# The last two batches' pages computed behind quad 34, sums in the order of completion, and four gathers a quad

## What is computed

```python
x = x + xattn(layernorm(x), ctx)
h = layernorm(x)                                  # 4096 tokens x 128
shared = silu(h @ sg_w.T) * (h @ su_w.T) @ sd_w.T
scores = sigmoid(h @ gate_w.T) + gate_bias        # 64 experts in 8 groups
# the 4 best groups, in them the 6 best experts, weights scaled to sum 1 -> comb
a = silu(einsum('th,eih->eti', h, eg_w)) * einsum('th,eih->eti', h, eu_w)
routed = einsum('eti,ehi,te->th', a, ed_w, comb)
out = x + shared + routed
```

## Time and profile before

| | us |
|---|---|
| median of the runs (592.63 to 596.7) | 593.04 |
| span of the profiled execution, first to last instruction | 792.4 |
| POOL busy in it | 389.3 |
| PE busy | 503.3 |
| DVE busy | 456.1 |
| ACT busy | 352.3 |

### The profile page before, as it was taken

One profiled execution on the slowest core, in us unless ns is written; L12 is line 12 of the kernel. 1 busy time (PEld: TensorE's weight loads), 2 busy tenths in 40 slices (PEclk: granted clock), 3 DMA queues, 4 the chain that ended last, 5 costly groups with the idle time before them and its releaser, 6 DMA issues.

```text
span 792.4 us, 12061 instructions
## 1 busy us (share of the span) xinstructions
PE 503.3 (64%) x3204; PEld 420.8 (53%) x3204; DVE 456.1 (58%) x2264; ACT 352.3 (44%) x962; POOL 389.3 (49%) x425
## 2 busy tenths in 40 slices
PE   3767555766555574632359956788688889777700
PEld 2445334444334343311359856778688789777700
DVE  6587556667555576656233624576776756346532
ACT  3564433344443343322215934466666766246400
POOL 2006445654455655556650055454554545555574
PEclk9885555555555555555568976899988876897555
DMA  7532123322123332223425533455455555654421
GB/s 195 194 113 94 62 100 107 104 100 98 47 80 107 107 100 98 95 78 129 124 81 134 148 94 95 106 138 151 126 145 137 151 137 146 160 153 107 113 70 47
DMA packets 98708, 90.60 MB, mean 114 GB/s; under 512 B 10576, under 2 KB 85456, under 8 KB 98640
## 3 DMA queue, kind: packets, MB, share of 16 engines
q1 hardware_dynamic: 85232, 64.26, 27.5%
q0 software_dynamic: 12288, 25.29, 11.3%
q10 hardware_dynamic: 1120, 0.28, 0.2%
HBM read 41.32 MB, written 48.46 MB: 113 GB/s over the span
## 4 chain that ended last, share of the span: by engine, by line
PE 30%; another core or an unknown queue 17%; issue 16%; ACT 14%; POOL 11%; DVE 9%; ACTq 2%; DMA 0%; POOLq 0%; DVEq 0%
PE bank_s L1155 14%; POOL pages L447 6%; PE bank_o L1155 4%; PE bank_q L1155 3%; PE bank_s L1151 2%; ACT d_now L511 2%; ACT p_t L533 2%; ACT pxt L511 2%; POOL empty L492 2%; ACT gu_now L511 2%; ACT k_exp L521 1%; ACT s_act L672 1%; POOL p_t L492 1%; PE bank_o L1151 1%
## 5 line engine op out<-in xcount | busy, mean ns | idle before, releaser
L1155 PE MATMUL bank_s<-pxt,gu_now 128*128 128x64 f32 x768 | 116.5, 316 | 51.6 <-ACT pxt L511 31.3
L492 POOL DMA_INDIRECT p_t<-results,place_i x96 | 91.1, 949 | 110.6 <-ACT s_act L672 72.8
L1155 PEld LDWEIGHTS bank_s<-pxt,gu_now 128*128 128x128 f32 x768 | 111.4, 231 | 58.1 <-ACT pxt L511 36.4
L492 POOL DMA_INDIRECT empty<-results,place_i x96 | 91.1, 949 | 77.2 <-issue 35.1
L1111 DVE TENSOR_TENSOR h_t<-bank_s,s_act 64x256 f32<-64x256 f32 x128 | 54.7, 427 | 113.9 <-ACT s_act L672 95.4
L447 POOL DMA_INDIRECT pages<-payload,place_i x96 | 93.0, 968 | 37.9 <-issue 27.0
L447 POOL DMA_INDIRECT pages<-payload_b,place_i x96 | 92.8, 967 | 35.8 <-issue 26.7
L437 POOL TENSOR_TENSOR rstd<-ve,minus_half 128x4 f32<-128x4 f32 (+1 forms) x21 | 18.6, 885 | 132.6 <-DVE ve L927 130.0
L672 ACT ACTIVATE s_act<-bank_s 64x512 f32<-64x512 f32 x64 | 37.8, 590 | 79.5 <-remote 36.0
L533 ACT ACTIVATE p_t<-bank_s 128x512 f32<-128x512 f32 x64 | 36.2, 598 | 67.9 <-issue 27.9
L1255 PE MATMUL bank_o<-bias_h,row_h 96*128 96x256 bf16 x16 | 6.1, 381 | 72.2 <-ACT o_t L511 70.3
(11 more groups left out here) (169 smaller groups left out, 1164.1 us busy)
## 6 DMA issues: line engine op xcount, KB each, us to landing
pg<-pages SPq DMA_DIRECT2D x64, 258.0 KB
results<-y_s SPq DMA_DIRECT2D x64, 256.0 KB
pages<-empty SPq DMA_DIRECT2D x21, 774.0 KB
w_gu<-in_expert_gu SPq DMA_DIRECT2D x16, 256.0 KB
w_d<-in_expert_d SPq DMA_DIRECT2D x31, 128.0 KB
out_x<-xb SPq DMA_DIRECT2D x16, 128.0 KB
xb<-in_x SPq DMA_DIRECT2D x3, 512.0 KB, 8.0
pages<-payload,place_i POOLq DMA_INDIRECT x96
```

What stands on the lines that cost most here:

```text
L492: pool.indirect_dma_start(out=ys[n % YS_SLOTS][:, k, :], out_offset=None, in_=results[0:landed * QUAD * P, :], in_offset=bass.IndirectOffs ...
L1155: return pe.matmul(dst, w, v, start=True, stop=True)
```

## The change

- Quads are now computed in another order. `quad_at(p)` gives the quad that stands at position p of the loop: positions 0 to 34 are quads 0 to 34, positions 35 to 48 are the fresh quads 50 to 63, and positions 49 to 63 are quads 35 to 49. Below, a *position* counts in the new order; in the kernel before, position and quad are the same.
- `landed_before(b)` says how many positions must be stored for batch b: 11 + 3b for batches 0 to 8 (11 to 35), 46 for batch 14, 49 for batch 15, and 52, 55, 58, 61, 64 for batches 9 to 13. `turn_of` sorts the batches by it: 0 to 8, 14, 15, 9 to 13. Gathers, sums, the shared expert and the stores of the output go in this order.
- Four gathers are tied to each quad in place of three, and a batch starts with the quad behind its last one: `gathers_from` is 12, 15, 18, ... 36 for batches 0 to 8, then 47, 50, 53, 56, 59, 62, 65. The sums of its two tiles stand behind the products at `gathers_from` + 3 and + 4.
- `pages` and `results` are two tables each, an old and a new one. The tables are filled with zeros in 22 DMAs as before, of other sizes (the old table's first has 8 pages, the new one's 8).

```diff
-FIRST_BEAT = FIRST_SUM - 6
-GATHERS_A_QUAD = TOPK // 2
+GATHERS_A_QUAD = 4
+FRESH_AT = 35
+FRESH_QUADS = NQ - SPLIT_QUAD
...
+        def quad_at(p):
+            if p < FRESH_AT:
+                return p
+            return p - FRESH_AT + SPLIT_QUAD if p < FRESH_AT + FRESH_QUADS else p - FRESH_QUADS
+
+        def landed_before(b):
+            n = quads_before(b)
+            if b >= SPLIT:
+                return n - SPLIT_QUAD + FRESH_AT
+            return n if n <= FRESH_AT else n + FRESH_QUADS
+
+        turn_of = sorted(range(B), key=landed_before)
+        gathers_from = []
+        for b in turn_of:
+            gathers_from.append(max(landed_before(b) + 1, gathers_from[-1] + TPB * TOPK // GATHERS_A_QUAD if gathers_from else 0))
+
+        def summed_at(p):
+            return [TPB * i + t for i in range(B) for t in range(TPB) if gathers_from[i] + 3 + t == p]
...
-                if q == SPLIT_QUAD:
+                if q == FRESH_AT:
                     pages_complete(B)
...
-                if q == FIRST_STORE + 2 * TPB * stored:
+                if q == gathers_from[stored] + 4 + STORE_BEHIND + 2:
                     store(stored)
...
-            def beat(step):
+            def beat(i, step):
                 q, part = divmod(step, GATHERS_A_QUAD)
+                q += gathers_from[i]
+                if q >= NQ:
+                    return
                 if part == 0:
                     pool.wait_ge(act_ready, q + 1)
                 elif part == 1:
+                    pool.wait_ge(pxt_ready, min(q + 2, NQ))
+                elif part == 2:
                     pool.wait_ge(h_ready, HALVES * (q + 1))
                 else:
                     pool.wait_ge(y_ready, q)
...
                 for k in range(TOPK):
-                    if GATHERS_A_QUAD * FIRST_BEAT + TOPK * n + k < GATHERS_A_QUAD * NQ:
-                        beat(GATHERS_A_QUAD * FIRST_BEAT + TOPK * n + k)
-                    pool.indirect_dma_start(out=ys[n % YS_SLOTS][:, k, :], out_offset=None, in_=results[0:landed * QUAD * P, :],
-                                            in_offset=bass.IndirectOffsetOnAxis(ap=place_i[:, n, k:k + 1], axis=0)
+                    beat(i, t * TOPK + k)
+                    pool.indirect_dma_start(out=ys[n % YS_SLOTS][:, k, :], out_offset=None, in_=done,
+                                            in_offset=bass.IndirectOffsetOnAxis(ap=place_i[:, tile, k:k + 1], axis=0)
...
             def combine_next(q):
-                n, odd = divmod(q - FIRST_SUM, 2)
-                if n >= 0 and not odd:
+                for n in summed_at(q):
                     combine(n)
...
-            for n in range((NQ - FIRST_SUM + 1) // 2, TPB * B):
-                combine(n)
+            for n in range(TPB * B):
+                if gathers_from[n // TPB] + 3 + n % TPB >= NQ:
+                    combine(n)
```

More of the change, by code:

```diff
@@ L81, with build @@
 POWER_AFTER = {}
-def build(nc, x, ctx_cols, wq, bq, wk, bk, wv, bv, wo, bo, gate_cols, gate_bias, expert_gu, expert_d, shared_gu, shared_d, out, pages, results):
+def build(nc, x, ctx_cols, wq, bq, wk, bk, wv, bv, wo, bo, gate_cols, gate_bias, expert_gu, expert_d, shared_gu, shared_d, out, old_pages, new_pages, old_results, new_results):
     with ExitStack() as ctx:
@@ L272, in quads_before, with quad_in, held @@
             return pages_before(b) // QUAD
-        def fills_before(b):
-            return 1 + (pages_before(b) - FIRST_FILL + FILL - 1) // FILL
-        def held(q):
+        def quad_at(p):
[13 more added lines that the diff above has]
+            return [TPB * i + t for i in range(B) for t in range(TPB) if gathers_from[i] + 3 + t == p]
+        def fills_before(b):
+            if b < SPLIT:
+                return 1 + (pages_before(b) - OLD_PAGES % FILL + FILL - 1) // FILL
+            return OLD_FILLS + 1 + (pages_before(b) - OLD_PAGES - NEW_PAGES % FILL + FILL - 1) // FILL
+        def quad_in(both, p):
+            q = quad_at(p)
+            new = q >= SPLIT_QUAD
+            at = q - SPLIT_QUAD if new else q
+            return both[new][at:at + 1, :, :, :]
+        def held(p):
+            q = quad_at(p)
             for start in (0, SPLIT_QUAD):
@@ L332, in prefill @@
             def prefill(k):
-                sp.wait_ge(prefilled, 16 * (k + 1))
-                sp.dma_start(fill_v[bass.ds(k, 1), :, :].rearrange("k p c -> (k p) c"),
-                             empty[:, :, :].rearrange("p r c -> p (r c)")).then_inc(prefilled, 16)
+                new = k >= OLD_FILLS
+                pages, i = (new_pages, k - OLD_FILLS) if new else (old_pages, k)
+                first = (NEW_PAGES if new else OLD_PAGES) % FILL
+                start = 0 if i == 0 else (first + (i - 1) * FILL) * P
+                rows = first if i == 0 else FILL
+                if k > 0:
+                    sp.wait_ge(prefilled, 16 * k)
+                sp.dma_start(pages[start:start + rows * P, :].rearrange("(p r) c -> p (r c)", p=P),
+                             empty[:, 0:rows, :].rearrange("p r c -> p (r c)")).then_inc(prefilled, 16)
             load_x(0)
@@ L446, in scatter @@
                 for k in range(first, after):
-                    pool.indirect_dma_start(out=pages[:, :], out_offset=bass.IndirectOffsetOnAxis(
+                    pool.indirect_dma_start(out=(new_pages if n >= SPLIT else old_pages)[:, :], out_offset=bass.IndirectOffsetOnAxis(
                         ap=place_i[:, TPB * n + t, k:k + 1], axis=0), in_=payload[n % 2][:, t, k, :],
@@ L481, in gather @@
             def gather(n):
-                landed = quads_before(n // TPB)
-                if n % TPB == 0:
+                i, t = divmod(n, TPB)
+                b = turn_of[i]
+                tile = TPB * b + t
+                done = (new_results[0:(quads_before(b) - SPLIT_QUAD) * QUAD * P, :] if b >= SPLIT
+                        else old_results[0:quads_before(b) * QUAD * P, :])
+                landed = landed_before(turn_of[i])
+                if t == 0:
                     for j in range(SLOTS):
@@ L1094, in combine @@
                         dve.wait_ge(added, (TOPK - 1) * n + k)
-                    part = dve.scalar_tensor_tensor(out=xt, in0=ys[n % YS_SLOTS][:, k, :], scalar=weight[:, n, k:k + 1], in1=xt,
+                    part = dve.scalar_tensor_tensor(out=xt, in0=ys[n % YS_SLOTS][:, k, :], scalar=weight[:, tile, k:k + 1], in1=xt,
                                                     op0=ALU.mult, op1=ALU.add)
```

45 lines of the change are left out of this document (23 added, 22 removed).

## The result

The change makes the kernel slower: 623.85 us (median of 4 runs, 621.08 to 626.69) against 593.56 us (4 runs, 592.63 to 596.7), a ratio of 1.0503 with a 95% interval of 1.045 to 1.0555, or +30.3 us. The profiled execution of the changed kernel took 625.98 us, with a span of 624.1.

A forecast was written before the change was run, and what follows sets the result against it. The prediction took POOL's indirect DMAs as the bound. Its second stage went from 249.5 to 276.7 us, +27 us; it took +20, between +27 and +12, so 593 + 20 = 613 us, range 583 to 622, likeliest case 602 to 620.

The forecast's parts named there:

- The bound: Whole kernel: POOL's indirect DMAs bind it, 192 scatters at 1.27 us and 192 gathers at 1.25 us.
- Balanced: Second stage of the kernel before: DVE and POOL both come to 250 us, the loop to 203 us.
- The gap: Between batches 8 and 14: POOL stands still from 136.3 to 163.5 us after the first gather, 27 us.
- the two upper ones: Second stage, two estimates of the loss: +27 us at the trace's spacing, +12 us at 1.15 us.
- an upper value: Second stage: the +27 us sum, called upper since the spacing without the profiler may be shorter.
- item 1 of the parts: End of the kernel: 16 gathers follow the last quad instead of 27; a time bound by POOL gains nothing.
- item 4: Behind the pause: 84 gathers, 105 us, to 276.7 us; other bound, 17 positions at 5.0 us, called lower.
- Item 5: Order, two tables, fills and two more waits in a group: taken as 0, between -2 and +2 us.
- The profiled span: Changed kernel's profile: the span may shrink by up to 16 us, even opposite to the median.
- Faster: Rival, loop and end: quads have slack, the gap costs nothing, only the end counts; 582 us, chance 0.23.
- Same: Rival, gap and end: spacing near 1.0 us, some DVE slack, the two cancel; 588 to 598 us, chance 0.2.
- Much slower: Rival, loop: POOL stalls reach DVE at once through the sums and add to the gap; 628 us, chance 0.07.

The follow-up runs named there:

- clean profile: The unchanged kernel before, profiled a second time with no edit: 596.98 us, span 595.1 us, no pause between first and last gather.

## Why the prediction was right and wrong

The direction and the mechanism, one pause of POOL at the seam in front of batch 14, held there by the sums, came out as forecast. The size lay 2 us above the range, and 10.9 above the forecast of 613.

- **The bound** was right: POOL's indirect DMAs, 1.25 and 1.27 us apart, fill the second stage. The clean profile gives 344 us ahead of the silu of quad 12 (343 forecast) and 595.1 - 344.33 = 250.8 us behind it (249.5). That it was read from a profile that ran 199 us too long worked because POOL's durations and its spacing without a wait were the same in both (a gather 949 ns, and 952 to 956), and its idle times were what was stretched. "Another core or an unknown queue", 17% of the first chain, isn't in the second chain at all.
- **"Balanced"** was a little off: the loop takes 197.7 us, where 203 was worked out, so POOL is the bound by at least 13 us and not by none. Most of the five are the held quads 49 to 56: the sum took 3.75 us for each, POOL's pace and not theirs, and they take 3.16.
- **The gap** was the right term and nearly the right size, 27 us against 29.8. It began 0.8 us later than worked out (POOL free at 480.45, 137.1 us behind the silu of quad 12; 136.3 forecast) and ended 3.4 us later (166.9; 163.5 forecast). Of the 3.4, the sum of position 40 gives 1.6: the later start, and a sum that starts 3.78 us behind the start of its last gather, where I had taken 2.6. The positions up to the silu of 46 give 2.8: 504.75 - 485.27 = 19.5 us in place of 16.7. The silus of 41 to 45 are 6.8, 4.8, 5.0 and 3.5 us apart. The first of these holds DVE's wait, and the next two are together 2.9 us above the 3.5 that I had for each; PE ran at the lower clock for a while there (a group of 16 matmuls took 3.68 us, then 2.00). From the silu of 46 to the gather it was 1.0 us less than forecast, with a landing of 3.1 us for the 4.8 taken from the stretched profile, and 0.8 us from landing to gather that weren't in the sum.
- **The step that failed** is the last one of the sum: "I take +20, between the two upper ones", because "the spacing without the profiler may be shorter". The sum with the trace's spacing was +27, or 620 us, and +30.3 was measured. I had no row that showed a shorter spacing, and the two that spoke of it (the median, and the sum of 593 that met it) spoke for 1.25. The clean profiles settle it: their spans are within 2 us of the measured times of the same executions, and in them the spacing is 1.26. Thus the spacing in the sum was mis-sized by a discount against the evidence, and with it the range's upper end, "an upper value", had no room for a sum that was itself a little short.
- **The end** (item 1 of the parts) was half right. That a time bound by POOL gains nothing there held. That 16 gathers would follow the last silu didn't: 28 do (36 before). POOL needs 5.0 us for what a position was to take with it, and the loop behind the pause runs ahead of it, so POOL carries its lag to the end. I had worked out this other bound myself in item 4, and then not used it for the count.
- **Item 5**, everything else for nothing, within 2 us either way, held: three gathers without ties leave 4.6 us, and their pause is 5.1. The waits on `pxt_ready` cost nothing at four gathers a quad. But ties aren't free in general: with three gathers and no arrears they cost some 17 us.
- **The profiled span** grew, and didn't shrink as I had thought it might; the stretch of the first profile belongs to that execution and not to profiling.
- **The rivals.** Faster, by slack in the quads: gone with the clean profile. Same, by a short spacing: gone with the spacing. Much slower, "held back by the sums": the sums' tie is real, and moving them gives 10.8 us back, but it works through the pause's length and not by stalls added to it. It named 628 us, the forecast 613; what was measured lies between them, nearer to this rival's number. But its added stalls aren't there: beside the one pause POOL has no idle time of over 0.7 us between its first and last gather, and the mechanism is the forecast's.

No version here with all its gathers beats the kernel before. Its POOL has no pause between first and last gather, so with this many gathers at this spacing it is the stages ahead that could give something. The 21 powers on POOL ahead of and between the scatters, 18.6 us, are a candidate; it wasn't tried, and nothing here shows what it would give.

## What to carry to other kernels

An engine that does equal operations with a fixed distance between them can be full at a low busy share, here 75%; multiply count by distance before you believe the busy shares. A schedule that gives such an engine more operations to each step of a loop doesn't make it faster: POOL made its gathers 1.26 us apart before and after. What moves is how early the loop asks for their results. Here DVE's sums came nine positions earlier, the loop had to wait there, and what POOL needed next wasn't ready, so POOL, the bound, stood still, and to within 2 us all of that was added to the time, wherever the seam lay. So before you move a consumer forward, work out when its producer will be done. And when a sum worked out from a trace meets the measured time, leave its durations alone: a discount needs a row of its own.

## What the runs showed that I had not expected

- A profiled execution can be far from its kernel: the first profile of the kernel before has a span of 792.4 us, the second 595.1, with the same number of instructions. What differs is idle time, and PE's busy time (503.3 against 444.4 us by their pages, at a mean granted clock of 0.675 against 0.766). What stretched the first one stays open.
- The granted clock of PE went with the stalls of the loop. In before's loop it is 1.00, the level of 2.4 GHz, throughout (345 to 542 us, above), and it is 1.00 from 344 to 482 us with three gathers and no ties. In the kernel after, where the sums make DVE wait, busy times by stage give less for the gathers ahead of the pause, the pause, and the gathers behind it:

```profile
core 0: us, PE busy (x) PEld busy (x) DVE busy (x) ACT busy (x) POOL busy (x), PEclk, DMA share, GB/s
344.00:480.00 136.00, 122.54 (x911) 117.66 (x909) 104.19 (x396) 90.09 (x268) 102.60 (x108) 0.89 0.65 170
480.00:510.00 30.00, 27.10 (x196) 25.80 (x195) 17.02 (x84) 22.42 (x70) 0.15 (x1) 0.83 0.50 132
510.00:616.00 106.00, 61.14 (x449) 57.46 (x448) 62.64 (x258) 53.02 (x168) 80.42 (x84) 0.76 0.51 134
```

  The means between 0.5 and 1 mix the two levels. From 489 to 494 us the clock is at 0.50, the level of 1.2 GHz, after the loop had waited for the sum of position 40. That is the stretch of the matmul group of 3.68 us. From 499 us on it is at 1.00 again:

```profile
489.00:494.00 5.00, 4.99 (x24) 0.50 0.19 52
...
499.00:505.00 6.00, 5.83 (x51) 1.00 0.67 177
```

  These two rows are of PE alone (PE busy, clock, DMA share, GB/s). PE's busy time over the whole run is 25 us longer than before's for the same 3204 matmuls. Most of it lies beside POOL's gathers and costs nothing there, since POOL doesn't wait; in the pause, where POOL waits for the loop, the stretch at the lower clock is that of the 2.9 us above. No run held the clock up, so this share of the pause is read from the spacing of the silus and not measured by itself.
- At the seam two landings stand on the path, one behind the other. The batch's last sum starts 3.8 us behind the start of its last gather. The store of the results lands 3.1 us after its issue, and the gather that waits for it starts 0.8 us later. At the end of the kernel before, second profile, the first of these is 2.5 us (586.05 to the last sum at 588.58); why it is longer in the loop stays open.
- Stages that no edit was meant to change move too: the silu of quad 12 comes between 339.6 and 344.6 us in the nine profiled executions of the kernels before and after and of the experiments. So a few us between two single spans say nothing, and the lengths above are taken from one event to another inside an execution.
